# Two of eight quads of nodes counted as one summed tile, and layer 1's first products inside layer 0

## The reference, cut to what matters

```
mask = (adj != 0)
rank = cumsum(mask, axis=1);  deg = rank[:, -1:];  k = minimum(deg, 100)
pos = rank - (deg - k)
w = mask * where(pos > 0, 0.5 ** (k - pos), 0.0)
x = layernorm(x + w @ (x @ W0) + b0)
h = x                                     # then twice, with its own weights:
    m = adj @ (h @ W); r, z, n = gates(m, h); h = relu((1 - z) * n + z * h)
x = layernorm(x + h)
x = layernorm(x + (dinv * (adj + I) * dinv) @ x @ W2)
x = layernorm(x + concat(x, (adj @ x) / (deg + 1)) @ W3.T)
```

## Time and profile before

| what | value |
|---|---|
| median of 3 runs | 471.95 us (471.89 to 473.51) |
| the profiled execution: time, span | 472.1 us, 470.3 us |
| mean granted TensorE clock | 0.993 |
| TensorE matmul busy | 448.9 us, 95%, 2374 instructions |
| ScalarE busy | 226.1 us, 48% |
| VectorE busy | 182.4 us, 39% |
| GpSimd busy | 113.3 us, 24% |
| adjT loads (GpSimd's queue) | 16.78 MB written, 35.6% of 16 DMA engines' span |
| share of the chain that ended last | PE 82%, DMA 6%, DVE 5% |

### The profile page before, as it was taken

One profiled execution on the slowest core, in us unless ns is written; L12 is line 12 of the kernel. 1 busy time (PEld: TensorE's weight loads), 2 busy tenths in 40 slices (PEclk: granted clock), 3 DMA queues, 4 the chain that ended last, 5 costly groups with the idle time before them and its releaser, 6 DMA issues.

```text
span 470.3 us, 6397 instructions
## 1 busy us (share of the span) xinstructions
PE 448.9 (95%) x2374; PEld 212.4 (45%) x2390; DVE 182.4 (39%) x694; ACT 226.1 (48%) x383; POOL 113.3 (24%) x155
## 2 busy tenths in 40 slices
PE   6989999999999999999999998999999999999992
PEld 1323333343334433446555554455455555455571
DVE  2220210043005500445544448776726434074454
ACT  3878788879887788335434433434211011100100
POOL 9112612007100300051121204324224232111011
PEclk9999999999999999999999999999999999999997
DMA  8999999999999970010110100000001101000000
GB/s 123 155 154 107 107 107 106 108 107 110 112 110 107 109 81 0 1 22 1 24 22 13 22 13 1 1 0 1 1 1 22 24 12 24 11 24 13 23 13 22
DMA packets 24894, 23.71 MB, mean 50 GB/s; under 512 B 14368, under 2 KB 16288, under 8 KB 24864
## 3 DMA queue, kind: packets, MB, share of 16 engines
q0 software_dynamic: 9360, 16.78, 35.6%
q1 hardware_dynamic: 15216, 6.33, 5.8%
q10 hardware_dynamic: 288, 0.20, 0.2%
HBM read 69.44 MB, written 1.05 MB: 150 GB/s over the span
## 4 chain that ended last, share of the span: by engine, by line
PE 82%; DMA 6%; DVE 5%; POOL 2%; issue 2%; ACT 1%; POOLq 0%; DVEq 0%
PE Y L743 40%; PE both L700 11%; PE both L702 10%; PE Y L670 10%; DMA adjT<-in_adjT 6%; PE both L652 2%; PE both L655 2%; PE both L647 1%; PE both L658 1%; PE both L660 1%; POOL adjT L242 1%; DVE m L430 1%; POOL rstd L214 1%; PE both L723 0%; DVE hrow L454 0%
## 5 line engine op out<-in xcount | busy, mean ns | idle before, releaser
L743 PE MATMUL Y<-adjT,S 128*128 128x512 fp8e4 (+1 forms) x1056 | 228.6, 373 | 1.3 <-POOL S L229 0.9
L312 ACT ACTIVATE wgt<-both 128x512 int16<-128x512 f32 x256 | 152.7, 597 | 31.9 <-PE both L702 15.4
L743 PEld LDWEIGHTS Y<-adjT,S 128*128 128x128 f16 x1056 | 102.7, 99 | 111.0 <-POOL S L229 1.4
L702 PE MATMUL both<-adjT,tri 128*128 128x512 fp8e4 x256 | 98.2, 384 | 0.0
L700 PE MATMUL both<-adjT,fix 128*128 128x512 fp8e4 x248 | 94.7, 382 | 2.9 <-DMA adjT<-in_adjT 2.0
L670 PE MATMUL Y<-wgt,S 128*128 128x512 bf16 x241 | 92.0, 382 | 0.0
L214 POOL TENSOR_TENSOR rstd<-stat,mhalf 128x4 f32<-128x4 f32 (+2 forms) x29 | 31.2, 1075 | 209.2 <-DVE stat L411 209.2
L700 PEld LDWEIGHTS both<-adjT,fix 128*128 128x128 bf16 x248 | 23.9, 96 | 80.2 <-ACT wgt L312 53.0
L293 ACT ACTIVATE yT<-Y 128x512 f32<-128x512 f32 (+1 forms) x17 | 9.7, 572 | 93.0 <-PE Y L743 53.6
L454 DVE TENSOR_TENSOR rz<-both,consts 128x512 f32<-128x512 f32 x4 | 2.8, 692 | 122.5 <-PE both L723 122.5
L242 POOL DMA_DIRECT2D adjT<-in_adjT x63 | 34.1, 595 | 62.7 <-DMA adjT<-in_adjT 62.6
(11 more groups left out here) (98 smaller groups left out, 329.9 us busy)
## 6 DMA issues: line engine op xcount, KB each, us to landing
adjT<-in_adjT POOLq DMA_DIRECT2D x63, 256.0 KB, 39.0
out_rows<-xrow SPq DMA_DIRECT2D x7, 128.0 KB, 1.9
xrow<-in_xrow SPq DMA_DIRECT2D x1, 640.0 KB, 8.3
hrow<-in_w_gates SPq DMA_DIRECT2D x1, 512.0 KB, 13.4
biases<-in_biases SPq DMA_DIRECT2D x1, 416.0 KB, 7.6
x<-S SPq DMA_TRANSPOSE x24, 2.4
xrow<-in_xrow SPq DMA_DIRECT2D x1, 256.0 KB, 4.2
adjT<-in_adjT POOLq DMA_DIRECT2D x2, 128.0 KB, 6.1
```

The costliest lines, as they stand in the source:

```text
L312: nc.scalar.activation(wgt[:, c, t % 2, :], V[c][:, :], ACT.Relu).then_inc(w_ready[c], 1)
L702: nc.tensor.matmul(V[c][:, :], tri[:, :], adj_tile(q, jb, c), start=False, stop=False, skip_group_check=True).then_inc(v_done[c], 1)
L743: mm = nc.tensor.matmul(Y[g % 2][:, 0:nb * P], S[layer % 2][:, jb, :], cols[:, jb, :], start=(jb == 0), stop=(jb == JB - 1), skip_group_ch ...
```

## The change

Two quads of every quarter, 6 and 3 (`MASKED`), are no longer counted tile by tile.

- The host reorders the nodes of these quads so that the four nodes next to each other in order lie on one partition, one in each tile (`placed`), in the matrix, in x and in the result.
- GpSimd adds the quad's four tiles, 128 x 1024 each, into one tile `dsum` (`sum_quad`, three additions). It does this in its loop over the loads, behind the issue of the load that stands one quarter after the quad's last one; in the last quarter behind all loads. `root` of a quarter moves from loop place 13 to loop place 6, and in the last quarter it stands between the two sums.
- TensorE counts `dsum` once (`tri_sum`, `fix_sum`) in place of four tiles, and ScalarE evicts it once, into `seen`. A quarter has 26 steps: 24 tiles and 2 quads.
- VectorE makes the four tiles' weights from `seen` (`mask_quad`): four instructions for the weights (L537 of the changed kernel) and three that pass the count on (L542), 128 x 1024, 16-bit and 8-bit operands, both in SBUF.
- TensorE multiplies these weights with the features at steps set by the table `MASKED_AT`. `combine(0, ...)` of the quarter before stands after step 5 in each of quarters 1 to 3, and VectorE's `rows0` and `split_rows0` stand ahead of both `mask_quad` there.
- In steps 17 to 25 of quarters 1 to 3 TensorE makes two products of layer 1 per tile jb that is ready (`FILL`), 16 a quarter: 48 in all, the first 24 tiles of units 0 and 1.
- There are four product banks instead of two (`bank`), and the order of layer 1 is written out (`layer1`), with units 2 and 3 in the places that units 0 and 1 had.

```
+MASKED = (6, 3)
+STEPS = []
+for quad in range(G - 1, -1, -1):
+    if quad in MASKED:
+        STEPS.append(("quad", quad))
+    else:
+        STEPS += [("tile", jb) for jb in range(quad * B + B - 1, quad * B - 1, -1)]
...
+        def bank(layer, g):
+            return Y[(layer * G + g + 2) % 4] if layer else Y[g % 2]
...
+            def sum_quad(q, quad):
+                e = q * NM + MASKED.index(quad)
+                first = q * JP + 2 * (G - 1 - quad)
+                for i in (first, first + 1):
+                    pool.wait_ge(load[i % NLOAD], 16 * (i // NLOAD + 1))
+                if e >= 2:
+                    pool.wait_ge(dsum_used, e - 1)
+                d = dsum[e % 2]
+                nc.gpsimd.tensor_tensor(d, adjT[:, q, quad * B + 3, :], adjT[:, q, quad * B + 2, :], ALU.add, saturate=False).then_inc(dsum_step, 1)
...
+                nc.gpsimd.tensor_tensor(d, d, adjT[:, q, quad * B, :], ALU.add, saturate=False).then_inc(dsum_ready, 1)
...
-                    if q >= 2 and n == 13:
+                    for quad in MASKED:
+                        late = 2 * (G - 1 - quad) + 1
+                        if q >= 1 and n == late:
+                            sum_quad(q - 1, quad)
+                    if q >= 2 and n == 6:
                         root(q - 2, 2 * B)
-            root(Q - 2, 2 * B)
+            for quad in MASKED:
+                sum_quad(Q - 1, quad)
+                if quad == MASKED[0]:
+                    root(Q - 2, 2 * B)
             root(Q - 1, 2 * B)
...
+                def weights(k, seen_now):
+                    if e >= 1:
+                        dve.wait_ge(masked_used, B * (e - 1) + B - k)
+                    nc.vector.scalar_tensor_tensor(out=wq[:, k, :], in0=seen_now, scalar=0.0, in1=a4[k], op0=ALU.max, op1=ALU.mult)\
+                        .then_inc(masked_ready, 1)
+                def pass_tile(k, seen_now, out):
+                    nc.vector.scalar_tensor_tensor(out=out, in0=a4[k], scalar=-float(STEP), in1=seen_now, op0=ALU.mult, op1=ALU.add)\
+                        .then_inc(seen_step, 1)
...
+            mask_quad(0, MASKED[0])
...
             for q in range(Q):
-                if q == Q - 1:
+                if q >= 1:
                     rows0(q - 1)
                     split_rows0(q - 1)
+                for quad in MASKED:
+                    if q >= 1 or quad != MASKED[0]:
+                        mask_quad(q, quad)
                 pick_degree(q, 0)
...
+            FILL = {17: (0, 1), 18: (2, 3), 19: (4, 5), 20: (6, 7), 21: (8,), 22: (9,), 23: (10, 11), 24: (12, 13), 25: (14, 15)}
+            MASKED_AT = {10: ((6, 3, 0),), 11: ((6, 3, 1),), 12: ((6, 2, 0),), 13: ((6, 2, 1), (6, 1, 0)), 14: ((6, 1, 1), (6, 0, 0)), 15: ((6, 0, 1),), 20: ((3, 3, 0),), 21: ((3, 3, 1),), 22: ((3, 2, 0), (3, 2, 1)), 23: ((3, 1, 0),), 24: ((3, 1, 1),), 25: ((3, 0, 0), (3, 0, 1))}
+            def slot(q, s):
+                if q >= 1 and s == 5:
...
+                    combine(0, 2 * q - 2)
+                    combine(0, 2 * q - 1)
+                for quad, k, c in MASKED_AT.get(s, ()):
+                    weigh_masked(q, quad, k, c)
+                for u in FILL.get(s, ()) if q >= 1 else ():
+                    jb = (q - 1) * 2 * B + u // 2
+                    product(1, u % 2, jb, jb + 1)
...
+            def layer1():
+                product(1, 2, 0, 7)
+                combine(0, G - 2)
+                combine(0, G - 1)
+                product(1, 2, 7, EARLY)
+                product(1, 3, 0, EARLY)
+                open_gates()
+                for g in range(3):
+                    product(1, g, EARLY, JB)
+                product(1, 3, EARLY, JB - 2)
+                combine(1, 0)
+                product(1, 3, JB - 2, JB)
+                product(1, 4, 0, 20)
+                combine(1, 1)
+                product(1, 4, 20, JB)
+                product(1, 5, 0, 8)
+                combine(1, 2)
+                product(1, 5, 8, 28)
+                combine(1, 3)
...
```

More of the change, by code:

```diff
@@ L108, in build @@
         identity = consts[:, 2 * P:3 * P]
-        Y = [ps(f"Y{c}", [P, GC]) for c in range(2)]
+        Y = [ps(f"Y{c}", [P, GC]) for c in range(4)]
         both = ps("both", [P, 2, B, 4 * D])
@@ new lines, in weigh_masked @@
+            def weigh_masked(q, quad, k, c):
+                e = q * NM + MASKED.index(quad)
+                if c == 0:
+                    pe.wait_ge(masked_ready, B * e + B - k)
+                    if q == 0 and k == B - 1:
+                        pe.wait_ge(s_ready, G - quad)
+                mm = nc.tensor.matmul(Y[c][:, :], S[0][:, quad * B + k, :], wq[:, k, c * GC:(c + 1) * GC].bitcast(BF16),
+                                      start=False, stop=False, skip_group_check=True)
+                if c == 1:
+                    mm.then_inc(masked_used, 1)
@@ new lines, in count @@
+            def count(q, c, s, which, stop=False):
+                kind, at = STEPS[s]
+                if kind == "tile":
+                    return nc.tensor.matmul(V[c][:, :], (tri, fix)[which][:, :], adj_tile(q, at, c), start=False, stop=stop,
+                                            skip_group_check=True)
+                e = q * NM + MASKED.index(at)
+                if which == 0:
+                    if e == 0:
+                        pe.wait_ge(const_ready, 10)
+                    pe.wait_ge(dsum_ready, e + 1)
+                mm = nc.tensor.matmul(V[c][:, :], (tri_sum, fix_sum)[which][:, :], dsum[e % 2][:, c * GC:(c + 1) * GC],
+                                      start=False, stop=stop, skip_group_check=True)
+                if which == 1 and c == 1:
+                    mm.then_inc(dsum_used, 1)
+                return mm
@@ L852 @@
     rows = r.results[0]["out_rows"]
-    return flat(rows.reshape(P, JB, D).transpose(1, 0, 2)).reshape(N, D)
+    rows = flat(rows.reshape(P, JB, D).transpose(1, 0, 2)).reshape(N, D)
+    return flat(placed(rows, 0, back=True))
```

230 lines of the change are left out of this document (143 added, 87 removed).

## The result

The changed kernel takes 512.37 us (median of 4 runs, 512.03 to 514.81), the kernel before 471.97 (471.89 to 473.51) beside it: a ratio of 1.086, interval 1.082 to 1.090. It is slower by 40 us; 505 was forecast, with a range of 479 to 514. The profiled execution took 512.29 us, its span is 510.5 us, 40.2 more than the 470.3 of before, and the mean granted clock is 0.947 instead of 0.993.

A forecast was written before the change was run, and what follows sets the result against it. TensorE was taken as the bound, with late starts on VectorE and GpSimd making it wait. Quarter 0 +8.0, quarters 1 to 3 -5.2 work and +30.0 waits, layer 1 +0.4: +33.2 us on 472.1, so 505, range 479 to 514.

The forecast's parts named there:

- The bound: Whole kernel: TensorE is the bound in layers 0 and 1, but average busy times don't show when moved work can start.
- Price of an addition and a mask: GpSimd's 1024-column addition 2.29 us, from a line through two float rows; VectorE's mask instruction about 1.22 us.
- Cheap additions: Rival, layer 0: an addition costs 0.61 us and a mask 0.69, giving +7 us, 479; chance 0.06.
- Quarter 0, +8.0: Layer 0, quarter 0: TensorE waits 10 and 6.6 us for GpSimd's sums; first pick at 63.6 instead of 55.59.
- Quarters 1 to 3, work -5.2, waits +30: Layer 0: 24 matmuls fewer and 16 products more a quarter; contending additions and masks cost 10.0 us of waits a quarter.
- The undisturbed wait: Quarters 1 to 3: TensorE waits at least 3.4 us for quad 6's first mask behind VectorE's rows, whatever GpSimd does.
- C: The combine's end in each of quarters 1 to 3; first weights were forecast at C + 14.3, or C + 9.9 without contention.
- 12.6: Rival, no contention: quarters 1 to 3 wait only 12.6 us in all, as additions and masks run together; 487.8, chance 0.18.
- The clock as a rival, +6.7: Rival, layer 0: new waits of 6 to 8 us drop TensorE to its lower clock level; +6.7 us, 512, chance 0.15.
- Layer 1, +0.4: Layer 1: a unit's loop of 7.5 us bounds it, so removing 48 products (10.4 us) gains nothing; +0.4 us.
- No change in layers 2 to 4: Layers 2 to 4: they keep their order and none of the banks' waits there is long; 0 us.
- TensorE's count decides: Rival, faster: VectorE and GpSimd keep ahead, so the removed matmuls are the gain; 456, chance 0.04.

The follow-up runs named there:

- the run with thin additions: The changed kernel with GpSimd's three additions of quad 3 in quarters 1 to 3 cut to 64 of 1024 columns: 490.26 us, ratio 1.039.

## Why the prediction was right, and where it was not

**The bound.** That the averages hide the start times held: TensorE lost busy time and the kernel grew by 40 us.

**Price of an addition and a mask.** Taken 2.29 us, measured 2.00 to 2.08 in quarter 0 (beside the second sum it was VectorE that was held up); the line through two 32-bit rows was 13% too high, and 8-bit operands bought little. A mask: 1.22 taken, 1.22 measured. Cheap additions (479) are out.

**Quarter 0, +8.0.** +8.6. The first wait was 10.09 (forecast 10), the second 2.84 (6.6). The second wait's difference has three parts in the rows: the additions are shorter by 0.8 us a sum, load 9's quad is seen at 35.5, not 36.1, and the 54 matmuls ahead took longer, since 11 of them ran at the lower level. The second sum was thus ready 1.4 us sooner than forecast, and from there to the first pick it took 2.0 us longer, 1.7 of them in 9 more slow matmuls. That two misses nearly cancel is luck.

**Quarters 1 to 3, work -5.2, waits +30.** The waits are 29.4 us in sum, 9.3, 9.3 with 2.0 and 0.6, and 8.2 where I had 7.8, 1.5 and 0.7 thrice. The sum fits better than its parts: the first wait of each quarter was longer and the later ones mostly missing, so that agreement to 0.6 us is partly luck. The undisturbed wait was forecast at 3.4, and the run with thin additions measured 3.4. The place of the contention was half wrong: I had the additions meet the masks, but they met `split_rows0` first, which stands ahead, and so the first weights came at C + 16.1, not 14.3, and the tiles behind them were rarely late. The Trainium skill (SBUF — State Buffer, Who interferes with whom) speaks of a lock for the whole instruction; the durations of 2.3 to 3.5 us beside additions of 2 agree, and by it 30 was right and 12.6 not. Quarter 2 was 4 to 6 us longer than its neighbours, since the first sum of the last quarter follows that of quad 3, with 3.2 us of load issues between, and meets more masks (3.97 and 3.02 us at 145 and 149), which I had not seen.

**The clock as a rival, +6.7 (chance 0.15).** It came as well, and is the term missing from the 505. The quarters 1 to 3 grew by 31.2; -5.2 and 29.4 leave 7.0 us, and 34 matmuls there ran 0.43 us apart instead of 0.217, 34 x 0.21 = 7.2. I had 1.3 a quarter and it is 2.4, as a wait for the second tile doesn't hide the slow spell but starts another (quarter 2). It was wrong to set this beside the likeliest case as an either-or: in every run, each wait of TensorE in layer 0 of 7.9 us or more brought it, and the earlier trace rows had shown the price. That 512 lies inside the range is owed to this rival. The Trainium skill (TensorE: Matmul & The Clock Gate, Part 1) says that an idle array falls back; the rows agree, with a granted clock of 0.50 behind the waits of 10.09 and 9.34 us.

**Layer 1, +0.4.** Measured from the last pick to the end: +0.4. The combines are 7.6 us apart (7.5 forecast), TensorE idle for 1.8 us (1.8). That the 10.4 us of products are paid in layer 0 was shown by moving them back: 12.1 us less. The 1.7 us beyond 10.4 lie behind the last pick; 1.2 of them come before layer 2 begins, where 0.4 was expected. Why it is more, no run shows.

**No change in layers 2 to 4.** Held: the +0.4 covers them.

**TensorE's count decides (456).** It needed the first weights before C + 6.5 and a loop below 5.7 us. With the masks moved up, the products back and no GpSimd addition, the reduced count does bring 10 us; in the change as made its conditions were missed by 9.6 and 1.9 us.

Not tried: a longer lead of the loads, which bound quarter 0 and the first sum of quarter 1, and other places for the second sum of quarter 2.

## What to carry to other kernels

Work that is moved from a bound engine to idle ones is worth what its start times allow: list for each moved step what stands ahead of it in its new engine's order, and when the bound engine asks for it. If two chains hang behind the same late step, moving one brings little of what both bring (3.4 and 10.1 us alone, 33.4 together here), so try the pair before dropping either. Long GpSimd additions with operands in SBUF stretched the masks and the other VectorE instructions with two sources in SBUF beside them, some with one too, ahead of the step in question as well; the same additions on a busier VectorE were the better choice.
